# Rotating the queries of all head groups before any scores, with one 96-wide position product per image column

## The reference, cut to what matters

```python
qkv = (x.reshape(B, L, dim) @ w_qkv + b_qkv).reshape(B, L, 3, nh, hd)   # B=4, L=1024, dim=384
q, k = rot(q), rot(k)                                  # rotary embedding over (w, h)
attn = einsum('bnqd,bnkd->bnqk', q, k) * scale
rel_h = einsum('bnhwc,hkc->bnhwk', q6, bias_h)         # q6: rotated q as (h, w, c)
rel_w = einsum('bnhwc,wkc->bnhwk', q6, bias_w)         # one 32 x 32 table per image column w
attn = attn + rel_h[..., :, None] + rel_w[..., None, :]
out = softmax(attn) @ v                                # then @ w_proj + b_proj, plus the residual
x = x + out
```

## Time and profile before

| what | value |
|---|---|
| median of 3 runs (lowest, highest) | 3094.75 us (3092.77, 3095.74) |
| the profiled execution: its own time, its span | 3094.16 us, 3092.4 us |
| PE (TensorE) busy | 2684.6 us, 87% |
| DVE (VectorE) busy | 2242.5 us, 73% |
| ACT (ScalarE) busy | 1614.7 us, 52% |
| POOL (GpSimd) busy | 1351.2 us, 44% |
| mean granted TensorE clock over the span | 0.968 of 2.4 GHz |
| first attention product to first scores, image 1 | 2047.98 to 2083.66 us |
| first attention product of image 2 | 2394.30 us |

### The profile page before, as it was taken

How to read it: one execution, slowest core, us unless ns; L and a number is a source line. 1 busy time by engine, 2 the same in 40 slices (tenths; PEclk the granted TensorE clock), 3 DMA queues, 4 the chain that set the end, 5 groups by cost and what they waited for, 6 DMA issues and landing times. The chain is left out here.

```text
span 3092.4 us, 40835 instructions
## 1 busy us (share of the span) xinstructions
PE 2684.6 (87%) x16088; PEld 1346.6 (44%) x16088; DVE 2242.5 (73%) x2157; ACT 1614.7 (52%) x1972; POOL 1351.2 (44%) x624
## 2 busy tenths in 40 slices
PE   5579788988889878687767999999999999999999
PEld 2134233333333333232322565555555565556555
DVE  0398988899888998899992566646665566646665
ACT  2464655555555556555541456625564356525564
POOL 1577887887778877788670200011000300011000
PEclk9799999999999999999996999999999999999999
DMA  2344544455444555445551210120120210120110
GB/s 78 108 142 129 163 150 144 150 140 168 165 145 148 142 170 167 154 160 140 197 172 36 76 36 18 39 75 1 36 56 14 63 36 22 35 76 1 35 36 22
DMA packets 93526, 297.03 MB, mean 96 GB/s; under 512 B 16172, under 2 KB 18872, under 8 KB 93208
## 3 DMA queue, kind: packets, MB, share of 16 engines
q1 hardware_dynamic: 93336, 294.43, 30.8%
HBM read 238.27 MB, written 23.07 MB: 85 GB/s over the span
## 5 line engine op out<-in xcount | busy, mean ns | idle before, releaser
L1599 POOL TENSOR_TENSOR arena<-arena 128x1024 f32<-128x1024 f32 x384 | 903.2, 2357 | 307.4 <-DVE arena L1081 297.7
L1081 DVE TENSOR_TENSOR_SCAN arena<-PS,arena 128x1024 f32<-128x1024 f32 x384 | 879.0, 2289 | 102.2 <-ACT PS L1442 70.9
L577 PE MATMUL PS<-arena,ident 128*128 128x512 f32 x1536 | 762.0, 620 | 15.0 <-ACT arena L1453 12.8
L1442 ACT ACTIVATE PS<-arena,a_inf,a_neg 128x1024 f32<-128x1024 f32 x384 | 463.8, 1208 | 586.3 <-DVE arena L1081 580.3
L1201 DVE CUSTOM_DVE_ANT_1 arena<-PS,arena 128x1024 f32<-128x1024 f32 x384 | 467.7, 1219 | 323.4 <-PE PS L880 321.8
L1526 ACT ACTIVATE arena<-arena,neg_max 128x1024 f32<-128x1024 f32 x384 | 441.0, 1148 | 494.8 <-DVE neg_max L1201 494.8
L1089 DVE TENSOR_TENSOR arena<-arena,PS 128x1024 f32<-128x1024 f32 x384 | 460.8, 1200 | 57.7 <-PE PS L568 56.4
L568 PE MATMUL PS<-arena,sel 96*128 96x512 bf16 x768 | 239.4, 394 | 295.5 <-DVE arena L1089 291.7
L1629 POOL TENSOR_TENSOR arena<-arena 128x512 f32<-128x512 f32 x48 | 68.4, 1425 | 955.2 <-ACT arena L1495 955.2
L880 PE MATMUL PS<-arena 64*128 64x512 f32 x1536 | 431.6, 640 | 19.3 <-DMA arena<-arena 12.8
L577 PEld LDWEIGHTS PS<-arena,ident 128*128 128x128 f32 x1536 | 302.5, 198 | 275.0 <-issue 221.4
(11 more groups left out here) (125 smaller groups left out, 2205.3 us busy)
## 6 DMA issues: line engine op xcount, KB each, us to landing
arena<-b_rows SPq DMA_DIRECT2D x256, 512.0 KB, 3.7
arena<-b_rows SPq DMA_DIRECT2D x256, 256.0 KB, 3.9
arena<-arena SPq DMA_DIRECT2D x192, 128.0 KB, 3.3
arena<-arena SPq DMA_DIRECT2D x120, 64.0 KB, 2.6
normed<-x_in SPq DMA_DIRECT2D x12, 512.0 KB, 5.4
residual<-x_in SPq DMA_DIRECT2D x12, 512.0 KB, 5.6
x<-residual SPq DMA_DIRECT2D x12, 512.0 KB, 5.3
xn<-residual SPq DMA_DIRECT2D x12, 512.0 KB, 4.7
```

Source lines behind the costliest of these rows:

```text
L577: last = pe.matmul(dst[:, half(h)], lhs, rhs[:, half(h)], start=start, stop=stop, skip_group_check=True)
L1081: dve.tensor_tensor_scan(HS[:, at % 2, ::step], DA[:, ::step], DBU[:, at % R3, ::step], 0.0, ALU.mult, ALU.add).then_inc(scan_done.sem, 1)
L1442: act.activation(DA, DELTA[:, tile % 2, :], ACT.Exp, bias=a_inf[:, col:col + 1], scale=a_neg[:, col:col + 1]).then_inc(da_ready.sem, 1)
L1599: pool.tensor_tensor(DBU[:, at % R3, :], DU[:, tile % 2, :], BSB[:, at % R3, :], ALU.mult).then_inc(dbu_ready.sem, 1)
```

## The change

The queries of all three groups are now projected and rotated first (halves 0 to 5), then the keys of group 0 (halves 6, 7), all in `START`. When the six query halves are ready, seven `rel` jobs make rel_w of all groups: one product for each image column with the three groups side by side, 96 wide, five columns to a job (32 products an image, where there were 64). The two `relh` jobs follow, and V comes last, unmixed. The steps of group 0 keep two `proj` jobs and four `relh` jobs; the four other `proj` jobs and the four `rel` jobs are gone from them. Keys now live in `X[:, 2, :]`, and rel_w of group 2 in `X[:, 0, :]`, so the load of the residual into `X` moves behind the last head loads. The waits follow from this: `scores` of steps 0 to 2 wait for V and the position results, GpSimd waits before it first writes keys.

```diff
-        RELC = from_mats(30, 2)
+
+        KEYS = X[:, 2, :]
+        RELC = [from_mats(30)[:, 0, :], from_mats(31)[:, 0, :], X[:, 0, :]]
...
-        PREPARED = [(0, "q"), (0, "k"), (1, "q"), (2, "q"), (1, "k"), (2, "k")]
...
+        PREPARED = [(0, "q"), (1, "q"), (2, "q"), (0, "k"), (1, "k"), (2, "k")]
+        JOBS = [[("proj", n) for n in range(8)] + [("rel", n) for n in range(REL_JOBS)] + [("relh", 0), ("relh", 1)],
+                [("proj", 8), ("proj", 9)] + [("relh", n) for n in range(2, 6)],
                 [("proj", 10), ("proj", 11)]]
...
+        START = [(m, ()) for m in range(len(JOBS[0]))] + [(None, range(QB))]
+
+        JOB_AT = [{4 + 4 * m: m for m in range(len(JOBS[1]))}, {6: 0, 10: 1}, {}]
...
             for b in range(B):
-                load_image(X[:, :, :], x1, b, x_loaded.sem)
...
-                for k, (ready, count) in enumerate(((rope_ready, 2), (rope_ready, 4), (rel_saved, 2))):
+                for k, (ready, count) in enumerate(((rope_ready, 2), (rope_ready, 8), (rel_saved, REL_JOBS))):
...
                 if b + 1 < B:
                     load_image(XN[:, :, :], xn2, b + 1, normed_loaded)
+                for loaded in head_loaded:
+                    sp.wait_ge(loaded.sem, loaded.after(b, HEAD_DMAS * GROUPS))
+                load_image(X[:, :, :], x1, b, x_loaded.sem)
...
-                        pe.wait_ge(rope_ready.sem, rope_ready.after(b, 2 if n < 2 else 8))
-                        part, groups, lines = (n, 1, IMG // 2) if n < 2 else (n - 2, 2, IMG // 4)
-                        grid = QKC[:, 0:2 * groups - 1:2, :].rearrange("p g (h w) -> p g h w", h=IMG)
...
+                        pe.wait_ge(rope_ready.sem, rope_ready.after(b, 2 * GROUPS))
+                        grid = QKC.rearrange("p g (h w) -> p g h w", h=IMG)
+                        for r, at in enumerate(range(n * LINES, min((n + 1) * LINES, IMG))):
+                            last = pe.matmul(dst[:, r * GROUPS * IMG:(r + 1) * GROUPS * IMG],
                                              W["rel_w"][:, 0, HG * (IMG - 1 - at):HG * (REL - at)],
                                              grid[:, :, :, at], start=True, stop=True, skip_group_check=True)
-                            if between and r % (lines // (CT * len(blocks) + 1)) == 1:
-                                value_product(*between.pop(0))
...
-                    if s == 1:
-                        pe.wait_ge(rel_saved.sem, rel_saved.after(b, 2))
+                    if s == 0:
+                        pe.wait_ge(v_saved.sem, v_saved.after(b, QB - 2))
+                    elif s == 1:
+                        pe.wait_ge(rel_saved.sem, rel_saved.after(b, REL_JOBS))
+                        pe.wait_ge(relh_saved.sem, relh_saved.after(b, 2))
+                    elif s == 2:
+                        pe.wait_ge(v_saved.sem, v_saved.after(b, QB))
...
+                        at = slice(n * LINES, min((n + 1) * LINES, IMG))
+                        src = src[:, 0:(at.stop - at.start) * GROUPS * IMG].rearrange("p (w g h) -> p g h w", g=GROUPS, h=IMG)
+                        for g in range(GROUPS):
+                            last = dve.tensor_copy(RELC[g].rearrange("p (h w) -> p h w", h=IMG)[:, :, at], src[:, g])
```

More of the change, by code:

```diff
@@ L356, in turned_place, with rotated @@
             return step_banks(2 * s + 3)
-        PREPARED = [(0, "q"), (0, "k"), (1, "q"), (2, "q"), (1, "k"), (2, "k")]
[L359 to L362, removed]
-                [("proj", 10), ("proj", 11)]]
[L366 to L371, removed]
+        PREPARED = [(0, "q"), (1, "q"), (2, "q"), (0, "k"), (1, "k"), (2, "k")]
+        JOBS = [[("proj", n) for n in range(8)] + [("rel", n) for n in range(REL_JOBS)] + [("relh", 0), ("relh", 1)],
+                [("proj", 8), ("proj", 9)] + [("relh", n) for n in range(2, 6)],
+                [("proj", 10), ("proj", 11)]]
+        def rotated(g, side):
+            return QKC[:, g, :] if side == "q" else KEYS
+        START = [(m, ()) for m in range(len(JOBS[0]))] + [(None, range(QB))]
+        JOB_AT = [{4 + 4 * m: m for m in range(len(JOBS[1]))}, {6: 0, 10: 1}, {}]
+        ROPE_FOR = [8, 10, 12]
         def job_bank(phase, m):
@@ L376, in last_use, with raw @@
         def last_use(n):
-            return n - 4 if n < 6 else n - 2
+            return n - 4 if n < 10 else n - 2
+        def raw(n):
+            return RAW[n % 4 if n < 8 else n % 2]
         LATE = [("sums", 0), ("norm", 0, 0), ("norm", 1, 0), ("sums", 1), ("norm", 0, 1), ("norm", 1, 1),
@@ L1119, in job @@
                     if kind == "proj":
-                        h, raw = n % 2, RAW[n if n < 4 else n % 2]
+                        h = n % 2
                         dve.wait_ge(raw_saved.sem, raw_saved.after(b, n + 1))
@@ L1124, in job @@
                             dve.wait_ge(rope_ready.sem, rope_ready.after(b, n - 1))
-                        dve.tensor_tensor(RT2[0:XT, h, :], raw[XT:P, :], W["sin"][XT:P, 0, half(h)], ALU.mult)
-                        dve.tensor_tensor(RT2[XT:P, h, :], raw[0:XT, :], W["sin"][0:XT, 0, half(h)], ALU.mult
+                        dve.tensor_tensor(RT2[0:XT, h, :], raw(n)[XT:P, :], W["sin"][XT:P, 0, half(h)], ALU.mult)
+                        dve.tensor_tensor(RT2[XT:P, h, :], raw(n)[0:XT, :], W["sin"][0:XT, 0, half(h)], ALU.mult
                                           ).then_inc(sin_done.sem, 1)
@@ L1494, in job @@
                     bias = COL["b_qkv"][:, g:g + 1] if side == "q" else bk_scaled[:, g:g + 1]
-                    act.activation(RAW[n if n < 4 else n % 2], banks(job_bank(phase, m), 1), ACT.Identity, bias=bias,
+                    act.activation(raw(n), banks(job_bank(phase, m), 1), ACT.Identity, bias=bias,
                                    scale=1.0 if side == "q" else ATT_SCALE).then_inc(raw_saved.sem, 1)
@@ L1628, in _ @@
                     pool.wait_ge(raw_saved.sem, raw_saved.after(b, n + 1))
-                    pool.tensor_tensor(RT1[:, h, :], RAW[n if n < 4 else n % 2], W["cos"][:, 0, at], ALU.mult
+                    pool.tensor_tensor(RT1[:, h, :], raw(n), W["cos"][:, 0, at], ALU.mult
                                        ).then_inc(cos_done.sem, 1)
```

41 lines of the change are left out of this document (18 added, 23 removed).

## The result

The changed kernel takes 3111.01 us, median of 4 runs (3106.20 to 3112.83), beside 3094.60 for the kernel before; the ratio is 1.0052, 95% interval 1.0038 to 1.0065. It is slower, as forecast, by 16.4 us, a little over half of the forecast 30. The profiled execution took 3112.83 us, with a span of 3111.0.

A forecast was written before the change was run, and what follows sets the result against it. TensorE bounds attention: start phase +14.4 us less 17.3 from the steps gives -2.9, the low clock +10.4, so +7.5 us an image, +30 in four: 3124 us. Own range 3114 to 3132; stated range 3090 to 3131.

The forecast's parts named there:

- TensorE bounds both phases, and what leaves the steps is worth its length: Start phase and steps: TensorE is the bound; four proj and four rel jobs leaving the steps save 17.8 us an image.
- Rotation gives the sixth query half at 24.7 us, TensorE waits 4.1: Start phase: rotation takes 3.35 us a half, so TensorE waits 4.1 us after its eight proj jobs.
- The third rival: Start phase: rotation slower, 3.92 us a half if whole instructions exclude one another, +1.7 us an image, 3131; chance 0.07.
- A 96-wide product costs 0.25 us: Position products, start phase: 0.125 us a record, 0.25 a product, 8.0 us for all 32 (7.3 to 8.7).
- The clock falls in the wait: Start phase: TensorE's granted clock falls to 0.50 in the 4.1 us wait for the sixth query half.
- It stays low over all position products, 8.0 us, and 2.75 behind them: Start phase: position products at half speed, +8.0 us, then 2.75 for the clock's return; +10.4 after taking off 0.3; chance 0.62.
- The second rival: Start phase: the clock falls but returns during the position products, costing 2.7 us; -0.2 an image, 3094; chance 0.18.
- Head loads are covered: Start of an image: all head loads landed by 50 us; at group changes, same issue rule as before, nothing charged.
- The 0.5 us for the first steps: First steps: fifth scores wait for ScalarE's copy of turned probabilities; 0.5 us charged, so 17.3 us remain saved.
- Sum: Attention of one image: -2.9 us without the clock, +10.4 for the clock, +7.5 in all.
- The sign: Whole kernel: slower, chance 0.72; same 0.17, faster 0.11.
- The forecast's turning point: Start phase clock: the change is faster than before only while the clock costs under 2.9 us an image.

The follow-up runs named there:

- the first experiment: The changed kernel with six V products moved from the end of the start phase to before the first position product: 3088.96 us, ratio 0.9986 to the kernel before.

## Why the prediction was right in sign and too large in size

- *TensorE bounds both phases, and what leaves the steps is worth its length.* Right. TensorE's time without waits between first scores and next image fell from 303.9 to 286.8 us in image 1, 17.1 where 17.8 was summed; where the 0.7 went no run shows.
- *Rotation gives the sixth query half at 24.7 us, TensorE waits 4.1.* Right to a tenth: 3.35 us a half, waits of 4.00 to 4.12. The third rival, whole instructions excluding one another, is out: at 3.92 a half it would have been 26.4. That instructions of the two engines overlap in part is all that 3.35 shows; that it is their fixed part, as the prediction says, no run shows.
- *A 96-wide product costs 0.25 us.* Wrong, 0.34: +2.8 us an image. The value was taken between a strided 64-wide product and a contiguous 128-wide one. The 64-wide strided one hid its own slow reading: 64 x 1.76 = 113 ns is just what its record took (0.114 us), and contiguous 96-wide records, whose columns don't bind, take 0.117 too, so the row could not tell which of the two, weights or columns, bounded it.
- *The clock falls in the wait.* Right, in every image. *It stays low over all position products, 8.0 us, and 2.75 behind them.* This is the step that failed: it came back after 5 to 6 us, within these products, and cost 1.2 us an image, not 10.4. The second rival had this course but a price of 2.7; it was less because at the low clock a 96-wide record takes 5.00 / 24 = 0.21 us against 0.169, only a quarter more, where the rival took the price of dense 512-wide ones. The rows on which the step rested, 2-wide products and the output products, were too far from 96 columns; with 64 and 32 the step's low clock holds in full.
- *Head loads are covered.* Right at the start of an image: the first scores don't wait. At the group changes the prediction said "the same rule as before" and charged nothing. The rule is the same, the cover was not: in the kernel before, two of the four `relh` jobs, 1.9 us, lay in SyncE's queue time, and the last load landed 0.85 us sooner after the first issue. This term was missing: the waits there grew by 3.0 us in image 1 (2.6 of them at the first change) and by 8.4 in all four. Why the loads were slower, no run tells. The 0.5 us for the first steps was right (0.47).
- *Sum* for image 1: -2.9 was forecast without the clock. +2.8 for the products, +1.2 for the clock, +3.0 for head loads, +0.7 for what left the steps, and 0.3 for small parts of the start phase give +5.1 an image, as measured. The growth of the head loads' waits differs from image to image: 2.8, 3.0, 0.3 and 2.3 us; in image 2 the clock also fell once behind them (2650.2 to 2653.6). With 0.8 us ahead of the attention the four images make the 18.6 us between the two profiled spans; the medians are 16.4 apart.
- *The sign* was right in part by luck. Errors of opposite direction largely cancelled: 9.2 us an image charged for a clock that came back, against 6.8 not charged for the products, the head loads, the steps and small parts. With the clock alone put right, the forecast would have been -2.9 + 1.2 = -1.7 an image, 7 us faster in four. The wait did what was said of it; that the change loses even so comes from the other terms.
- *The range.* Its upper end follows from the terms given; the lower one, with 7.3 for the products and 2 for the return, comes to 3116 and not 3114. The measured time lies below either; the stated range, 3090 to 3131, holds it because it takes in the second rival.
- *The forecast's turning point*, that the change is faster if the low clock is avoided, is borne out by the first experiment in sign, but only just (0.9986). By the prediction's terms it should have been 2.9 + 3.9 = 6.8 us an image, 27 in four, since the wait is filled too; 5 were measured. Product price (11), head loads (8) and steps (3) took the rest.

## What to carry to other kernels

When the stream of the bounding engine gets a new wait, look for work behind it that needs nothing of it, and put that first; here two lines of order were worth 22 and 11 us. Work that seems to be freely movable may be the cover of a queue elsewhere: before moving a job, read what the bounding engine would wait for at its old place, in DMA issues times their length. A price taken from a row that is bound by another resource (weights) is a lower bound for the wider operation, not its price.

## What the runs showed of the hardware that was not expected

- Under a long row of 64- and 32-wide float32 products, with a weight load for each record, TensorE's granted clock fell to 1.2 GHz 3 to 6 us into the row, behind waits of under 0.3 us and with TensorE busy throughout, and stayed there for 20 to 24 us, through the `relh` products behind them. Under the same data as 96-wide products it kept 2.4 GHz, and a clock lowered beforehand rose during them. The kernel before had the same narrow products in short groups between V products or score steps, and its clock held. Merging them was therefore worth 3143 - 3089 = 54 us in this order of work. By the price of before, 14.5 against 10.8 us an image, about 15 of these are the products themselves; the other 39, an estimate from these numbers, are the clock.
- A moving operand of 32-token runs at a stride of 128 bytes costs 1.76 ns a column at full clock (0.169 us for 96); contiguous, 96 columns take 0.117 us a record. At 1.2 GHz a strided record took 0.21 us at 96 columns (24 in 5.00 us) and as much in the mean over 64 and 32 (128 in 27.4 us).
- Behind waits of 1.85 to 2.01 us between score steps the clock fell for about 3 us in four places of the first experiment's profile, and not behind a wait of 1.86 us in the same profile, nor behind the longest of the changed kernel, 2.63 us at 1855.97. A different number of such falls in each execution would fit the spread of 10 us among the ten runs, whose longest has a mean granted clock of 0.964 and whose shortest 0.969; where the clock fell is known only for the profiled one.
